# Where a macaron layer gathers the late rows of its first FFN while the attention runs

## What is computed

```
x = x + 0.5 * ffn(layernorm(x))
x = x + attention(layernorm(x))
x = x + 0.5 * ffn(layernorm(x))
```

## Time and profile before

| | |
|---|---|
| median of three runs | 2252.35 us |
| the profiled execution | 2254.53 us, its span 2252.7 us |
| mean granted clock of TensorE | 0.931 |
| TensorE (PE) busy | 1973.1 us, 88% |
| VectorE (DVE) busy | 1512.3 us, 67% |
| ScalarE (ACT) busy | 1418.6 us, 63% |
| GpSimd (POOL) busy | 1141.4 us, 51% |
| the 64 late gathers | 65.1 us of GpSimd, started from 509.6 to 841.0 us |

### The profile page before, as it was taken

One profiled execution on the slowest core, in us unless ns is written; L12 is line 12 of the kernel. 1 busy time (PEld: TensorE's weight loads), 2 busy tenths in 40 slices (PEclk: granted clock), 3 DMA queues, 4 the chain that ended last, 5 costly groups with the idle time before them and its releaser, 6 DMA issues. The chain is left out here.

```text
span 2252.7 us, 47984 instructions
## 1 busy us (share of the span) xinstructions
PE 1973.1 (88%) x15384; PEld 1360.8 (60%) x15384; DVE 1512.3 (67%) x4290; ACT 1418.6 (63%) x2784; POOL 1141.4 (51%) x1582
## 2 busy tenths in 40 slices
PE   4839999859999999999999999999999787679982
PEld 3627778625555556666666666666666465558862
DVE  7937767746667667767766776767677387546773
ACT  3727777626666657767766777767676366547762
POOL 0756406446566564445434443444442057777774
PEclk9969999958999999999999999999999799789996
DMA  5564788678888888889888888988887122567794
GB/s 150 181 211 149 229 279 291 231 196 239 229 239 243 231 227 243 247 239 251 252 238 246 256 250 237 259 239 238 245 259 206 52 69 88 171 217 269 260 336 153
DMA packets 296958, 498.05 MB, mean 221 GB/s; under 512 B 43780, under 2 KB 199556, under 8 KB 296708
## 3 DMA queue, kind: packets, MB, share of 16 engines
q1 hardware_dynamic: 238932, 310.09, 48.6%
q0 software_dynamic: 55040, 183.75, 25.0%
q10 hardware_dynamic: 2736, 1.13, 0.2%
HBM read 252.71 MB, written 214.68 MB: 207 GB/s over the span
## 5 line engine op out<-in xcount | busy, mean ns | idle before, releaser
L1584 DVE CUSTOM_DVE_ANT_0 at_junk<-at_ps_s,at_rel 128x512 bf16<-128x512 f32 x1024 | 664.6, 686 | 227.6 <-PE at_ps_s L1111 214.0
L1299 ACT ACTIVATE at_probs<-at_ps_t 128x512 f32<-128x512 f32 x1024 | 558.9, 599 | 77.6 <-PE at_ps_t L1096 65.6
L1308 ACT COPY at_src<-at_ps_r 128x512 f32<-128x512 f32 x512 | 301.9, 590 | 355.6 <-PE at_ps_r L1127 249.3
L1096 PE MATMUL at_ps_t<-tab_ident,at_rel 128*128 128x128 f32 x2560 | 404.3, 290 | 0.0
L606 POOL DMA_INDIRECT rows_x<-ffn_sent_or_back,rows_index x256 | 268.5, 1049 | 212.1 <-ACT ffn_sent_or_back L558 134.7
L1141 PE MATMUL at_ps_v<-at_probs,at_v 128*32 128x256 f32 x4096 | 336.0, 400 | 0.2 <-ACT at_probs L1299 0.2
L1096 PEld LDWEIGHTS at_ps_t<-tab_ident,at_rel 128*128 128x128 f32 x2560 | 279.5, 144 | 71.3 <-issue 5.4
L1111 PE MATMUL at_ps_s<-at_ks,at_qs 31*128 31x512 f32 x1024 | 315.9, 510 | 5.1 <-DVE at_mx L1584 2.3
L1083 PE MATMUL at_ps_t<-at_qs,at_ks 32*128 32x256 f32 x2048 | 275.9, 298 | 6.1 <-DMA at_qs<-at_mrow 3.5
L1111 PEld LDWEIGHTS at_ps_s<-at_ks,at_qs 31*128 31x128 f32 x1024 | 122.7, 187 | 249.8 <-DVE at_mx L1584 144.9
L851 DVE TENSOR_TENSOR ffn_h<-ffn_silu,ffn_ps_gate 128x512 f32<-128x512 f32 x248 | 170.0, 686 | 153.2 <-ACT ffn_silu L577 151.9
(11 more groups left out here) (232 smaller groups left out, 3485.7 us busy)
## 6 DMA issues: line engine op xcount, KB each, us to landing
at_band<-at_src POOLq DMA_DIRECT2D x192, 574.0 KB
at_rel<-at_band SPq DMA_DIRECT2D x512, 143.5 KB
ffn_w_expert<-rows_w SPq DMA_DIRECT2D x92, 768.0 KB, 6.1
at_band<-at_src POOLq DMA_DIRECT2D x64, 512.0 KB
ffn_xg<-rows_x SPq DMA_DIRECT2D x46, 258.0 KB
ffn_xg<-rows_x SPq DMA_DIRECT2D x46, 256.0 KB, 4.7
rows_y<-ffn_y SPq DMA_DIRECT2D x46, 256.0 KB, 6.4
at_rel<-at_band SPq DMA_DIRECT2D x64, 128.0 KB
```

The costliest lines, as they stand in the source:

```text
L1096: ins = pe.matmul(ps_t[:, i, HALF * n + P * l:HALF * n + P * (l + 1)], rel[:, c % RREL, l, 2 * hp + i, kb * P:(kb + 1) * P], ident[:], sta ...
L1299: act.activation(probs[:, kp, 2 * hp + i].rearrange("p n q -> p (n q)"), ps_t[:, i, :], ACT.Exp).then_inc(exp_done.sem, 1)
L1308: act.copy(src[:, l, 2 * hp:2 * hp + 2, 0:BAND], ps_r[:, :, 0:BAND]).then_inc(qr_out.sem, 1)
L1584: dve.tensor_tensor_reduce(out=junk[:, i, :], in0=ps_s[:, i, :], in1=rel[:, c % RREL, l, h, :], scale=1.0, scalar=-3e38, op0=ALU.add, op1= ...
```

## The change

The gathers are no longer issued in pairs at the end of slots 0 to 31, but one by one in chosen places of slots 0 to 45. A place is (slot of the eight, half): half 0 stands after `fill_far(c + 3)` and before `send_band(c + 4, 0)`, half 1 at the slot's end. `GATHERED_AT` lists the places of the 64 gathers, `ADDED_AT` the slots in which a piece is added: the one after its second gather, and never two in one slot. These are slots 1, 2, 3, 6, 7, 9, 10, 11, 13, 14, 16, 17, 18, 19, 22, 23, 25, 26, 27, 29, 30, 32 to 35, 38, 39, 41, 42, 43, 45 and 46. `LATE_AT` becomes 48.

```diff
-    LATE_ROWS, LATE_AT = slice(EARLY_TILES * QPB, Q), PIECES + 2
+    GATHER_PLACES = ((0, 0), (0, 1), (1, 0), (1, 1), (2, 0), (2, 1), (4, 0), (5, 0), (5, 1), (6, 0), (7, 1))
+    GATHERED_AT = [(c, half) for c in range(ITEMS) for half in range(2) if (c % PER, half) in GATHER_PLACES][:2 * PIECES]
+    ADDED_AT = {}
+    for late_piece in range(PIECES):
+        ADDED_AT[max(GATHERED_AT[2 * late_piece + 1][0] + 1, max(ADDED_AT, default=0) + 1)] = late_piece
+    LATE_ROWS, LATE_AT = slice(EARLY_TILES * QPB, Q), max(ADDED_AT) + 2
+    assert LATE_AT + 2 < PER * (EARLY_TILES - 2) + NORMALISE_SLOT
...
-            def gather_late(p):
+            def gather_late(p, i):
 
                 t, two, k = EARLY_TILES + p // 4, p % 4 // 2, p % 2
-                late_added.wait(pool, p - RL, 1)
-                for i in range(2):
-                    numbers = rows.back[:, t // 2, k, t % 2 * QPB + 2 * two + i, :]
-                    pool.indirect_dma_start(late[:, p % RL, i, :], None, routed,
-                                            bass.IndirectOffsetOnAxis(numbers, 0)).then_inc(late_in[p % RL], 16)
+                if i == 0:
+                    late_added.wait(pool, p - RL, 1)
+                numbers = rows.back[:, t // 2, k, t % 2 * QPB + 2 * two + i, :]
+                pool.indirect_dma_start(late[:, p % RL, i, :], None, routed,
+                                        bass.IndirectOffsetOnAxis(numbers, 0)).then_inc(late_in[p % RL], 16)
 
             def slot(c):
                 if item(c + 3) is not None:
                     send_band(c + 3, 1)
                     fill_far(c + 3)
+                if (c, 0) in GATHERED_AT:
+                    gather_late(*divmod(GATHERED_AT.index((c, 0)), 2))
                 if item(c + 4) is not None:
                     send_band(c + 4, 0)
...
-                if 0 <= c < PIECES:
-                    gather_late(c)
+                if (c, 1) in GATHERED_AT:
+                    gather_late(*divmod(GATHERED_AT.index((c, 1)), 2))
...
-                    if k == 3 and 0 <= c - 1 < PIECES:
-                        add_late(c - 1)
+                    if k == 3 and c in ADDED_AT:
+                        add_late(ADDED_AT[c])
```

## The result

| | before | after |
|---|---|---|
| median of four runs | 2254.31 us (2249.9 to 2267.24) | 2233.97 us (2232.48 to 2234.86) |
| profiled execution (span) | 2254.53 (2252.7) us | 2234.21 (2232.4) us |
| TensorE busy | 1973.1 us | 1967.6 us |
| mean granted clock | 0.931 | 0.932 |

The ratio is 0.990, with an interval of 0.9858 to 0.9941: 20 us faster. The whole of it lies in the attention. From the first cast of `at_mrow` to the last it took 1255.7 us and takes 1235.8; ahead of it the kernel is 1.8 us longer, behind it 2.3 us shorter.

A forecast was written before the change was run, and what follows sets the result against it. TensorE was taken as the bound, 98.6% busy in the ten groups from 915.4 us. Gains of 25.2 us less 2, 2 and 1.2 made 20: 2254.5 to 2234.5, median about 2233; range 2226 to 2240, with rivals 2223 to 2250.

The forecast's parts named there:

- The two stalls go: First and sixth stretches, groups 1 to 3: lateness behind slots 6 and 3 goes; 5.9 us a group, 17.7 gained.
- Group 4's first stretch: Behind the gathers of slots 30 and 31: 14.58 us against 9.54 in group 7; 4.5 us gained.
- Group 0: The opening group, same two stalls but a low clock at its beginning: 3 us gained.
- The new places: Gathers moved to GpSimd's idle time before sends, tightest at (1, 0) and (4, 0): 2 us lost, 0 to 16.
- the waits: GpSimd waits for VectorE's add before six gathers; three late by 0.5 us: 2 us in the sum, at most 8.
- the longer stage: Slots 32 to 46 now hold 20 gathers: 1.2 us allowed for clock drops, 0 to 5.
- The additions: VectorE's adds of late rows, four a group, cost 1.9 us; moved, none removed, so 16 cost what they did.
- The late statistics: Moved from slot 34 to 48: up to 2.2 us leaves group 4, paid in group 6; net nothing, -1 to +1.
- the stall that stays behind slot 4: Rival, 17%: band write behind slot 3's work stays late, only the first stretch gains; 10.5 us, 2242.
- The slower rival: GpSimd's DMA queue, 5%: a gather ahead of a band write delays its landing; 23 us slower, 2275.
- what I had named as signs: Groups 77 to 80 us; first and sixth stretches some 10 us at clock 1.00; copy waits shrink; six waits under 1.5 us.
- Three signs of being wrong: Copies waiting over 2 us in slots 1, 3, 5, 0; 1.2 GHz beyond slot 31; landings over 5.5 us behind a gather.

The follow-up runs named there:

- second trace of the changed kernel: The changed kernel, unaltered, run again on chip C beside the kernel before: 2241.3 us, ratio 0.9907.
- the lighter kernel: The changed kernel with three late buffers, bias addition moved from slot 3 to 5, slot 6's normalisation split: 2229.0 us, 0.9849 of the kernel before.
- the pairs: The changed kernel with gathers in pairs at slot ends again, but never of slots 3 and 6: 2238.5 us, 0.9926 of the kernel before.

## Why the prediction was right

2233 us were forecast for what measured 2233.97, faster, within the range. The mechanism was right. That the total came within a microsecond was luck, as the steps show, by the profiled executions:

- **The two stalls go** (forecast 5.9 us a group in groups 1 to 3, 17.7). The groups lost 254.70 - 235.25 = 19.5 us, net of the costs at the new places. That the lateness at the two ends is what cost is shown by the two kernels that clear one end each and by the one that puts a single gather back at each of them.
- **Group 4's first stretch** (4.5): 14.58 to 9.65, 4.9 us. **Group 0** (3): 83.60 to 81.06, 2.5 us.
- **The new places** (2, at most 16), **the waits** (2, at most 8) **and the longer stage** (1.2): 5.2 us together were counted. Without the waits the six groups are between 1.0 us longer and 0.6 us shorter, without the gathers 1.4 to 3.0 us shorter. These three terms were too dear, by 2 to 4 us. Of the waits, three sends late by 0.5 us each were worked out, 1.5 us; four were late, by 2.2 us together, half of it in slot 42.
- **The additions** (1.9 us for four with statistics): kept, 9.95 and 9.94 us in stretch 4. Their size is between 3 and 7 us for all 16, where I had 7.6.
- **The late statistics** (net nothing): group 6 went from 77.7 to 79.3 us, which fits the 1.1 to 2.2 us that were to be paid there. Its second stretch alone doesn't show it: 12.20 us at a clock of 0.86, where the kernel before, with no such statistics in it, has 11.88 at the full clock.
- **Not in the sum:** the attention from group 6 on, which the change hardly touches, went from 758.56 to 763.19 us, 4.6 us more, by TensorE's busy time (747.40 to 754.94). 497.1 - 472.7 = 24.5 us gained in the first six groups, less 4.6, plus 0.5 outside the attention, is the 20.3 us of the span. Some 2 us of either figure is the statistics that moved over. The total was so close because a gain counted 2 to 3 us too small and a loss of about as much that was left out cancel, by chance.

Of the rivals, the stall that stays behind slot 4 is refuted as the rule: TensorE's idle time there is 0.11 to 0.12 us in groups 1 to 4. In the second trace of the changed kernel it came once, 1.11 us in group 3 (12.36 us). And the low clock came back in groups 1, 2 and 4 (12.03, 11.87 and 12.06 us), in the second trace in groups 3 and 4, where I had expected 1.00 and about 10 us. The slower rival, a longer landing behind a gather, did not decide; a small form of it may be real (below).

Of what I had named as signs, the first stretches (9.1 to 9.7 us at the full clock in groups 1 to 4) and the lengths of these groups (76.1 to 80.3 us) came as said, and the sixth stretches only in part. Three signs of being wrong showed, of which none overturns the account: ScalarE waited 2.7 us for the band in slot 3, but does so for 2.4 us in the kernel without gathers too; stretches partly at the low clock stand beyond slot 31, but in the kernel before as well (the first of groups 8, 9 and 13, at 0.85); and single landings behind a gather took over 5.5 us.

The gain itself has two parts of like size. In the first six groups TensorE's idle time fell from 497.14 - 474.99 = 22.2 us to 472.65 - 462.30 = 10.4, which is 11.8 us, and its busy time by 12.7 us for the same 4304 matmuls: the waits, and the time at 1.2 GHz that followed them.

## What to carry to other kernels

Small work on an engine that is half idle was nearly free or dear here by its place in that engine's queue: write down the idle time ahead of each instruction that others wait for, and put the work where that exceeds its duration, never behind the fullest stretch. The same table of a stage without the added work tells where the engine's own work could move too; here one move out of the fullest slot paid. In a kernel bound by TensorE a wait can cost more than its own length, by the clock that falls behind it: 1.65 us of idle time stand in a stretch of 13.41 us whose like in group 7 takes 9.54.

## What the runs showed that I had not expected

- **The clock falls in stretches without a stall.** TensorE is idle for 0.11 us in the sixth stretch of group 4 of the kernel after, and its clock there is 0.86. Groups 6 to 15, in which the kernels hardly differ, took from 750.6 to 765.7 us in their traces. Not all of this need be chance: the six traces without the late statistics in group 6 have 750.6 to 759.2 us, and the eight with them 760.5 to 765.7, but for the lighter kernel's 751.3. The four lowest without them are all of chip A, so what the later statistics cost beyond the 1.6 us of group 6 is open. On two chips the kernel whose gathers stand singly in every half slot has medians of 2239.4 and 2251.7 us, 0.992 and 0.995 of the kernel before. A change of 10 us wants its comparison on one chip.
- **A landing behind a gather is perhaps some tenths of a microsecond longer.** Where ScalarE waited for the band, the write had landed 5.5 us after its start as a median (77 writes), and 5.8 us where a gather had started within 3 us ahead of it (4 writes); in the second trace of the changed kernel 5.4 (80) and 6.1 us (8). This is one of them, 855.68 - 849.65 = 6.03 us, in slot 35 behind the gather of slot 34:

```profile
846.97 1.02 POOL L1454 DMA_INDIRECT at_late<-rows_y,rows_back  x1 [0.17 <-issue]
...
849.65 0.74 POOL L1393 DMA_DIRECT2D at_band<-at_src  x1 [0.55 <-POOL at_src L1386]
...
855.68 0.59 ACT L1314 COPY at_src<-at_ps_r 128x512 f32<-128x512 f32 x1 [1.03 <-DMA at_band<-at_src]
```

  Twelve writes don't settle it. Two of the traces with gathers have the landing of every band write. In the lighter kernel's, of the writes of slots 0 to 47, the 26 that started within 3 us behind a gather took 5.67 us as a median and the 69 others 5.08; against writes of the same place in the later groups it is 0.4 us more. In that of the pairs it is 4.79 (30) and 5.18 us (64), and 0.1 us more by place. So a delay is possible and not shown, and it is a fraction of the gather's own 4.0 us to landing. The Trainium skill ("DMA: Bandwidth & Descriptors", section "SWDGE vs HWDGE vs iDMA") says that for GpSimd's DMAs only one queue is allocated; a small delay would go with that, and no run here shows that it comes from there.
- **One gather there still costs, and less surely.** With a single gather at the end of slot 3 and none ahead of its second send, the sixth stretches of groups 1 to 5 take 10.14, 10.91, 12.68, 12.73 and 11.55 us on chip B and 10.39, 10.99, 12.75, 13.17 and 13.10 on chip C; with two they take 11.36, 13.89, 14.22 and 14.15 in groups 1 to 4. The band write there had no reserve to begin with the earlier trace rows.
